# Triangle layers on one core: the first projection with fp32 turned rows and one fp32 product in column quarters, in place of three fp16 products

## The reference

```
x0 = _gn(x)                                              # group norm over all positions
a = sigmoid((x0 @ Wa1 + ba1) * (x0 @ Wa2 + ba2))          # [512, 512, 16]
b = sigmoid((x0 @ Wb1 + bb1) * (x0 @ Wb2 + bb2))          # [512, 512, 16]
g = sigmoid(x0 @ Wg + bg)
z = einsum('bikc,bkjc->bijc', a, b)
x = x + g * (_ln(z, ln2_g, ln2_b) @ Wz + bz)
# second layer: layer norm, two gated projections with a mask, two triangle
# products, layer norm, and again a gated projection that is added to x
```

## Time and profile before

| | us |
|---|---|
| median of 3 runs | 5023.39 (5017.31 to 5030.55) |
| profiled execution, its own time | 5046.03 |
| its span, first to last instruction | 5044.3 |

### The profile page before, as it was taken

How to read it: one execution, slowest core, us unless ns; L and a number is a source line. 1 busy time by engine, 2 the same in 40 slices (tenths; PEclk the granted TensorE clock), 3 DMA queues, 4 the chain that set the end, 5 groups by cost and what they waited for, 6 DMA issues and landing times. The chain is left out here.

```text
span 5044.3 us, 90362 instructions
## 1 busy us (share of the span) xinstructions
PE 4064.9 (81%) x26438; PEld 2297.6 (46%) x26438; DVE 4109.2 (81%) x5835; ACT 3366.2 (67%) x4752; POOL 2717.9 (54%) x1426
## 2 busy tenths in 40 slices
PE   0004888893799999879999999989998886888888
PEld 0002555451455555545555555555553333444444
DVE  5888888688788888879999999867778887777777
ACT  0004999754677777658888888746666666888887
POOL 0000000093677777757777777743334435888887
PEclk9999999996899999989999999999999998999999
DMA  6996888653999999968888888776676757999999
GB/s 269 368 373 263 322 321 320 230 175 125 324 355 356 355 354 353 332 234 310 308 309 311 312 309 309 260 254 225 225 238 236 237 195 296 408 406 405 402 403 367
DMA packets 700450, 1532.72 MB, mean 304 GB/s; under 512 B 32800, under 2 KB 50656, under 8 KB 697952
## 3 DMA queue, kind: packets, MB, share of 16 engines
q1 hardware_dynamic: 632800, 1397.68, 78.3%
q10 hardware_dynamic: 67584, 134.23, 6.9%
HBM read 1009.59 MB, written 522.19 MB: 304 GB/s over the span
## 5 line engine op out<-in xcount | busy, mean ns | idle before, releaser
L1634 POOL TENSOR_TENSOR s_oT<-s_gated,s_x1t 128x1024 f32<-128x1024 f32 x256 | 689.6, 2699 | 223.5 <-DVE s_gated L1553 218.5
L888 POOL TENSOR_TENSOR s_x1T<-s_gz,s_xT 128x512 f32<-128x512 f32 x512 | 652.4, 1274 | 202.9 <-DVE s_gz L854 199.8
L1321 PE MATMUL s_y_ps<-s_ab 128*128 128x512 f16 x3072 | 698.0, 385 | 66.3 <-DVE s_ab L1391 64.7
L1026 POOL TENSOR_TENSOR s_low<-s_xc,s_high 128x1024 f16<-128x1024 f32 x256 | 547.8, 2140 | 265.0 <-ACT s_high L989 263.8
L795 PE MATMUL s_g_ps<-s_xT,s_Wg 128*128 128x512 f32 x1024 | 523.7, 593 | 0.0
L634 POOL MEMSET s_total<- 128x2048 f32 x1 | 1.8, 1810 | 960.4 <-POOLq L41 960.4
L854 DVE SCALAR_TENSOR_TENSOR s_gz<-s_z_ps,k_z_bias,s_g 128x512 f32<-128x512 f32 x512 | 384.1, 750 | 164.4 <-ACT s_g L821 162.1
L1321 PEld LDWEIGHTS s_y_ps<-s_ab 128*128 128x128 f16 x3072 | 301.4, 99 | 426.6 <-issue 94.9
L821 ACT ACTIVATE s_g<-s_g_ps,s_bg 128x512 f32<-128x512 f32 x512 | 352.0, 687 | 191.4 <-PE s_g_ps L795 191.4
L1553 DVE SCALAR_TENSOR_TENSOR s_gated<-s_p_ps,k_po_bias,s_gate 128x1024 f32<-128x1024 f32 x256 | 328.6, 1284 | 176.4 <-ACT s_gate L1590 147.7
L1295 POOL TENSOR_TENSOR s_at<-s_at,s_mask 128x1024 f32<-128x1024 f32 x64 | 164.2, 2566 | 502.2 <-DMA s_bt<-h_d 502.2
(11 more groups left out here) (215 smaller groups left out, 9695.3 us busy)
## 6 DMA issues: line engine op xcount, KB each, us to landing
s_xt<-in_x SPq DMA_DIRECT2D x128, 1024.0 KB, 6.9
s_xt<-in_x SPq DMA_DIRECT2D x256, 512.0 KB
x_d<-s_x1T SPq DMA_DIRECT2D x128, 1024.0 KB, 8.8
s_xt<-x_d SPq DMA_DIRECT2D x128, 1024.0 KB, 8.7
h_d<-s_h SPq DMA_DIRECT2D x128, 1024.0 KB, 6.4
s_x1t<-x_d SPq DMA_DIRECT2D x128, 1024.0 KB, 13.8
out<-s_ot ACTq DMA_DIRECT2D x128, 1024.0 KB, 9.3
s_mask_b<-mask_d SPq DMA_DIRECT2D x128, 512.0 KB, 4.3
```

The source lines that it names most:

```text
L888: pool.tensor_tensor(x1T[:, i // U, i % U, :], gz[:, i % 4, :], xT[:, i % 8, :], ALU.add).then_inc(added, 1)
L1026: pool.tensor_tensor(low[:, n % 4, :, :], xc[:, n % 4, :, :], high[:, n % 4, :, :], ALU.subtract).then_inc(rest_ready, 1)
L1321: last = pe.matmul(y_ps[:, ib, 0:N], ab[:, u % 2, 0, a, kb, ib * P:(ib + 1) * P], ab[:, u % 2, 1, b, kb, :], start=m == 0, stop=m == len(t ...
L1634: pool.tensor_tensor(oT[:, n % 4, :, :], gated[:, n % 4, :, :], x1t[:, n // 2, 2 * (n % 2):2 * (n % 2) + 2, :], ALU.add).then_inc(added, 1)
```

## The change

Stage 2 keeps the turned rows once, as fp32, in `xT`; the tiles high and low and their split weights go out of the stage. The work of a group is now:

- TensorE turns two rows at a time into one of three PSUM slots of two banks (`SLOTS` = 3); half h = 0 of a group goes to ScalarE, h = 1 to VectorE.
- ScalarE keeps rows 0 and 1 in one instruction of 128x1024 (`keep`, L435 of the changed file), VectorE rows 2 and 3 in another (L481).
- TensorE makes one fp32 product for each row and factor, in column quarters as before: 4 for m=0, 4 for m=1 (L404). Weights are `Wab4`, fp32.
- `open_first`, `multiply` and `sigmoid` keep their shapes.

With three PSUM slots of two banks, six banks hold turned rows, and `p_ps` has two banks, one for each factor, with no second one for the next group. So product m=0 waits for `open_first` of the group before it (`opened`), and product m=1 for `multiply` of the group before it (`gated`). GROUPS is 6 rather than 8 (21 turns' worth and a tail of two groups), `xT` has 6 places, the stores go in units of 3 groups.

```diff
-    CB, U, GROUPS = N // P, 4, 8
+    CB, U, GROUPS, SLOTS = N // P, 4, 6, 3
...
-        high, low = s.sbuf("high", [P, 4, U, N], FP16), s.sbuf("low", [P, 4, U, N], FP16)
+        xT = s.sbuf("xT", [P, GROUPS, U, N])
...
-        x_ps = s.psum("x_ps", [P, U, BANK])
-        p_ps = s.psum("p_ps", [P, 2, 2, BANK])
+        x_ps = s.psum("x_ps", [P, SLOTS, 2, BANK])
+        p_ps = s.psum("p_ps", [P, 2, BANK])
...
-                    pe.wait_ge(rest_ready, r * BODY + (U * g + j + 1))
-                    for q in range(CB):
-                        last = pe.transpose(x_ps[:, j, q * P:(q + 1) * P], xt[:, g % GROUPS, j, q, :], K.ident[:])
+                    k, n = g % GROUPS, (2 * g + h) % SLOTS
...
+                    pe.wait_ge((kept_dve, kept_act)[h], r * GROUPS + (g + 1))
+                    for j in range(2):
+                        for q in range(CB):
+                            last = pe.transpose(x_ps[:, n, j, q * P:(q + 1) * P], xt[:, k, 2 * h + j, q, :], K.ident[:])
...
-                    pe.wait_ge(rest_ready, r * BODY + (U * g + U + U))
-                    pe.wait_ge(gated, r * GROUPS + (g + 1))
-                    half = slice(32 * m, 32 * m + 32)
-                    for weights, part, start, stop in ((K.Wab_high, high, True, False), (K.Wab_low, high, False, False),
-                                                       (K.Wab_high, low, False, True)):
-                        for j in range(U):
-                            last = pe.matmul(p_ps[32 * j:32 * j + 32, g % 2, m, 0:N], weights[:, half], part[:, g % 4, j, :],
-                                             start=start, stop=stop)
+                    pe.wait_ge(kept_act, r * GROUPS + (g + 2))
+                    pe.wait_ge(kept_dve, r * GROUPS + (g + 3))
+                    if m == 0:
+                        pe.wait_ge(opened, r * GROUPS + (g + 1))
+                    else:
+                        pe.wait_ge(gated, r * GROUPS + (g + 2))
+                    for j in range(U):
+                        last = pe.matmul(p_ps[32 * j:32 * j + 32, m, 0:N], K.Wab4[:, m, 32 * j:32 * j + 32], xT[:, g % GROUPS, j, :],
+                                         start=True, stop=True)
...
-                def step(r, g, last=False):
-                    for j in range(U):
-                        if not (last and g + 2 >= GROUPS):
-                            turn(r, g + 2, j)
-                        if j % 2 == 1 and not (last and g + 1 >= GROUPS):
-                            product(r, g + 1, j // 2)
+                def step(r, g, end=None):
+                    for h in range(2):
+                        if end is None or g + 2 < end:
+                            turn(r, g + 2, h)
+                        if end is None or g + 1 < end:
+                            product(r, g + 1, h)
...
             @block.scalar
...
+                def keep(r, g):
+                    act.wait_ge(turned, r * PAIRS + (2 * g + 1))
+                    act.wait_ge(done, r * PAIRS + (2 * g + 2))
+                    act.activation(xT[:, g % GROUPS, 0:2, :], x_ps[:, 2 * g % SLOTS, :, 0:N], ACT.Copy,
+                                   scale=K.gn_scale[:]).then_inc(kept_act, 1)
...
+                def step(r, g, end=None):
                     sigmoid(r, g)
+                    if end is None or g + 3 < end:
+                        keep(r, g + 3)
+                    if end is None or g + 2 < end:
+                        open_first(r, g + 2)
...
             @block.vector
...
+                def keep(r, g):
+                    dve.wait_ge(turned, r * PAIRS + (2 * g + 2))
+                    dve.wait_ge(done, r * PAIRS + (2 * g + 2))
+                    dve.tensor_scalar(xT[:, g % GROUPS, 2:4, :], x_ps[:, (2 * g + 1) % SLOTS, :, 0:N], K.gn_scale[:], None,
+                                      ALU.mult).then_inc(kept_dve, 1)
...
-                    for j in range(U):
-                        if not (last and g + 2 >= GROUPS):
-                            rest(r, g + 2, j)
-                        if j == 1:
-                            multiply(r, g)
+                def step(r, g, end=None):
+                    if end is None or g + 2 < end:
+                        keep(r, g + 2)
+                    multiply(r, g)
```

More of the change, by code:

```diff
@@ L361, in _ @@
                     for k in range(GROUPS):
[L362 to L366, removed]
+                        reload(r, k)
+                    for half in range(2):
+                        store(r, half)
+                for k in range(REST):
+                    reload(REPS - 1, k)
                 for half in range(2):
                     store(REPS - 1, half)
+                store(REPS, 0, REST)
                 for half in range(2):
-                    sp.wait_ge(stored[half], REPS * 16 + 16)
+                    sp.wait_ge(stored[half], (REPS + 1 - half) * 16 + 16)
             @block.tensor
@@ L374, in _ @@
                 for m in range(2):
-                    pe.matmul(p_ps[:, m, 0, 0:1], K.Wab4[:, m, :], K.gn_shift[:], start=True, stop=True).then_inc(shifted, 1)
+                    pe.matmul(p_ps[:, m, 0:1], K.Wab4[:, m, :], K.gn_shift[:], start=True, stop=True).then_inc(shifted, 1)
                 pe.wait_ge(folded, 2)
[L377 to L382, removed]
-                    pe.wait_ge(rest_ready, r * BODY + (U * g + j + 1))
-                    for q in range(CB):
-                        last = pe.transpose(x_ps[:, j, q * P:(q + 1) * P], xt[:, g % GROUPS, j, q, :], K.ident[:])
+                pe.sem_inc(done, 2 * GROUPS)
@@ L406, in _ @@
                 for g in range(2):
-                    for j in range(U):
-                        turn(0, g, j)
+                    for h in range(2):
+                        turn(0, g, h)
                 for m in range(2):
@@ L413, in _ @@
                         step(r, g)
-                for g in range(GROUPS):
-                    step(REPS - 1, g, last=True)
+                for g in range(TAIL):
+                    step(REPS - 1, g, TAIL)
             @block.scalar
@@ L427, in open_first @@
                 def open_first(r, g):
-                    act.wait_ge(done, r * (2 * GROUPS) + (2 * g + 1 + 8))
+                    act.wait_ge(done, r * PAIRS + (2 * g + 1 + 2 * GROUPS))
                     act.wait_ge(gated, r * GROUPS + (g + 1))
-                    act.activation(first[:, g % 2, :], p_ps[:, g % 2, 0, 0:N], ACT.Identity, bias=bias[:, 0:1]).then_inc(opened, 1)
+                    act.activation(first[:, g % 2, :], p_ps[:, 0, 0:N], ACT.Identity, bias=bias[:, 0:1]).then_inc(opened, 1)
@@ L432, in sigmoid @@
                 def sigmoid(r, g):
+                    k = g % GROUPS
                     act.wait_ge(gated, r * GROUPS + (g + 1 + 2))
[L434 to L439, removed]
-                        if not (last and g + 2 >= GROUPS):
-                            round_high(r, g + 2, j)
-                        if j == 1 and not (last and g + 1 >= GROUPS):
-                            open_first(r, g + 1)
-                    sigmoid(r, g)
@@ L449, in _ @@
+                keep(0, 0)
+                keep(0, 1)
                 act.wait_ge(folded, 2)
                 open_first(0, 0)
+                keep(0, 2)
+                open_first(0, 1)
                 with act.Fori(0, REPS - 1) as r:
@@ L453, in _ @@
                         step(r, g)
-                for g in range(GROUPS):
-                    step(REPS - 1, g, last=True)
+                for g in range(TAIL):
+                    step(REPS - 1, g, TAIL)
             @block.vector
             def _(dve):
-                dve.sem_inc(rest_ready, U)
+                dve.sem_inc(kept_dve, 2)
                 dve.sem_inc(gated, 2)
@@ L462, in _ @@
                     dve.wait_ge(shifted, m + 1)
-                    dve.tensor_tensor(bias[:, m:m + 1], p_ps[:, m, 0, 0:1], K.bias4[:, m:m + 1], ALU.add).then_inc(folded, 1)
+                    dve.tensor_tensor(bias[:, m:m + 1], p_ps[:, m, 0:1], K.bias4[:, m:m + 1], ALU.add).then_inc(folded, 1)
                 dve.wait_ge(folded, 2)
[L466 to L469, removed]
+                def keep(r, g):
[3 more added lines that the diff above has]
+                                      ALU.mult).then_inc(kept_dve, 1)
                 def multiply(r, g):
-                    dve.wait_ge(done, r * (2 * GROUPS) + (2 * g + 2 + 8))
-                    dve.wait_ge(opened, r * GROUPS + (g + 1))
+                    dve.wait_ge(done, r * PAIRS + (2 * g + 2 + 2 * GROUPS))
+                    dve.wait_ge(opened, r * GROUPS + (g + 2))
                     dve.wait_ge(sig, r * GROUPS + (g + 1))
-                    dve.scalar_tensor_tensor(gate[:, g % 2, :], p_ps[:, g % 2, 1, 0:N], bias[:, 1:2], first[:, g % 2, :],
+                    dve.scalar_tensor_tensor(gate[:, g % 2, :], p_ps[:, 1, 0:N], bias[:, 1:2], first[:, g % 2, :],
                                              ALU.add, ALU.mult).then_inc(gated, 1)
```

(15 more changed lines are left out.)

39 lines of the change are left out of this document (22 added, 17 removed).

## The result

| | before | after |
|---|---|---|
| median, us | 5026.97 (5017.31 to 5074.11, 4 runs) | 5376.88 (5371.07 to 5380.03, 4 runs) |
| profiled execution, us | 5046.03 | 5377.4 |
| its span, us | 5044.3 | 5375.7 |
| granted clock of TensorE, mean | 0.972 | 0.959 |

The changed kernel is slower: ratio 1.0663, 95% interval 1.0626 to 1.07. That is +350 us, where 5600 us (+577) was predicted. The time lies inside the stated range, but outside the forecast's own (5540 to 5640) and nearest, 103 us off, to the rival in which all column quarters run abreast (5274 us).

A forecast was written before the change was run, and what follows sets the result against it. ScalarE was taken to set stage 2's pace at 4.06 us a group; transposes 1.02 and 1.09, two products of 2.24 and 2.00 idle make 8.59, stage 2 +576, the kernel 5600 us; range 5255 to 5660.

The forecast's parts named there:

- the rival in which all column quarters run abreast: Stage 2, TensorE: an fp32 product takes 0.96 us, a group 6.03 us, the kernel 5274 us; chance 16%.
- The old bound goes: Stage 2: ScalarE needs 2.43 us a group and VectorE 1.95, both far under the 4.06 us before.
- The added wait: Stage 2, TensorE: product m=1 waits for VectorE's keep and multiply, idling 2.00 us in every group.
- The fp32 product: Stage 2, TensorE: quarters' passes overlap only in part, so a product takes 2.24 us, against 0.75 before.
- starts keep the order: TensorE's queue: no matmul starts ahead of an earlier one, so passes stagger and end at 2.135 us.
- a rival in which it falls for good: Stage 2: TensorE's clock halves, products add over 530 us more, the kernel takes above 6100 us; chance 2%.
- The sum: Stage 2: 8.59 us a group, 126 groups plus both ends make 1096 us instead of 520, +576.
- The side: Whole kernel: slower by more than 0.3%, given 0.98; within 0.3% 0.01, faster 0.01.

The follow-up runs named there:

- e1: Changed kernel with VectorE's multiply of group g placed ahead of keep of group g+2; 5033.05 us, ratio 0.9988 to the kernel before.
- e3: Changed kernel with two PSUM slots for turned rows and four product banks, VectorE's order kept; 5034.78 us, ratio 0.9982 to the kernel before.
- e4: Changed kernel with all four rows' products written to column quarter 0, so a and b are wrong; 6076.3 us, one run.
- e6: Kernel before the change with a product's two loops swapped, each row's three fp16 terms one behind the other; 5055.74 us, ratio 1.002.
- e5: Changed kernel with two useless full-width fp32 products on TensorE between the second transposes and the waiting product m=1; 5294.56 us, two runs.
- e7: Changed kernel with xT in fp16 and one fp16 term replacing the fp32 product, a and b less exact; 5352.19 us, one run.
- e2: Changed kernel with multiply ahead of keep on VectorE, and TensorE doing both transpose halves, then both products; 4991.85 us, ratio 0.9904 to before.

## Why the prediction was right, and where it was off

The side and the cause, an added wait, were right. That the time lies in the stated range owes something to luck: the forecast's own 5540 to 5640 us missed it, and the range holds it only because it was stretched to a rival that I gave 16%.

- *The old bound goes.* Right: ScalarE is busy 37% of the window (under 35% was predicted, from longer groups). `keep` on VectorE took 1284 ns, which lies at the upper bound of 1280, and I had 1200. By the rule of the Trainium skill, "VectorE: DVE Perf Modes", on why PSUM operands drop a tier, the 840 ns fell away; this trace agrees, with 1284 ns for 1024 elements from PSUM.
- *The added wait.* Right, by e1 and e3 each alone. Its size was 2.13 us where the sum had 2.00; 0.08 of the difference is `keep`'s, and 0.06 is the step from VectorE's end to TensorE's start (706.51 - 706.36 = 0.15 us where I had 0.09).
- *The fp32 product.* This step failed. I had the starts keep the queue's order and a product take 2.24 us. It takes 703.29 - 702.29 = 1.00 us, and two of them stand in each group. The two passes of 0.43 us were right, e4 shows them one by one in 3.6 us. What was wrong is "starts keep the order": e6 shows a quarter's matmul started ahead of six earlier ones. The rule of the Trainium skill, "TensorE: Matmul & The Clock Gate", The mechanism, that matmuls start in program order, doesn't hold between column quarters here: e6 measured otherwise, and the measurement decides. The one of the Trainium skill, "TensorEngine Tiling (Array Packing)", Key Properties, that tiles operate independently, does. I had 0.96 us for that case, and gave it 16%. The rows of before could not tell the two apart, since neighbours in that queue always named different quarters; I read "each row fits it" as evidence, when each row fitted both.
- *The clock.* Priced only as a rival in which it falls for good (2%). It falls in 46 groups of 127, which are 1.57 us longer each: 72 us, and e5 takes 72.5 us off the same stretch.
- *The sum with measured terms.* A group at full clock: 6.24 us where the rival's had 6.03, over 126 groups +26. 5274 + 26 + 72 = 5372 us, against 5377 measured. Two slips in the recorded sum change nothing in this: its four blocks of transposes and two products ahead of the first group add up to 8.6 us and not 8.1, and the rows show one table load in each loop turn where it counts two (the trace has the other one, at L436).
- *The side.* Slower in every case that I gave a real chance; the wait alone sufficed. A group at full clock takes 6.24 us with the wait and 4.04 without it (e1): 2.13 us of idle time and 0.07 of the transposes' end that the next product no longer covers. Over 126 groups that is 277 us, and with the clock's 72 it is 349 of the 350 lost, because without the wait the two kernels are equal (e1).

## What to carry to other kernels

When buffers are shared out anew, follow for each single one who must have read it and what stands ahead of that reader in its own queue: here one line's place on VectorE was worth 344 us, and moving it (with the blocks on TensorE joined) turned a loss of 7% into a gain of 1%. An arrangement that relieves the fullest engine gains nothing if it makes a serial chain whose round takes longer than that engine did: here from TensorE to VectorE and back, 6.24 us a group against 4.06. And when several readings of the hardware fit all rows, their chances should be close to each other until a row tells them apart.

## What the runs showed of the hardware

- Matmuls for different column quarters started independently of their order in the queue: fp16 terms nested either way take the same 0.78 us (e6), and four fp32 products of 512 columns, eight passes, take 1.00 us including the change-over, against 3.55 in one quarter (e4).
- TensorE's clock fell to 1.2 GHz in part of the groups when TensorE idled 2.13 us in each group of 6.24 (granted 0.91), of 11.3 (0.91, e4) and of 4.9 (0.61, e7), and never in the middle of the stage with 0.41 us of idle time in 6.24 (e5) or at most 0.1 (e1, e2, e3). The kernel before kept 1.00 with TensorE idle for 10% of the window. What sets how often it falls stays open: e4 idled the smallest share of its time of the three, and 78 of its 127 groups took 13.0 us.
